# A reordered front for an embedding, interaction and MLP kernel: ids sent out by DMA broadcast from half 1 on, and new places for half 1's work

## The reference

```python
e = jnp.stack([tbl_0[ids[:, 0]], ..., tbl_15[ids[:, 15]]], axis=1)      # (2048, 16, 16)
# A = r_x0 with each of its 39 rows repeated 16 times, Bm = e stretched over the 39 rows (256 values over 39*16 places)
z = jnp.einsum('bnh,bnd,nk,khd,kd->bkh', A, Bm, alpha, w, hv[..., 0])   # (2048, 16, 16)
h = jnp.concatenate([z.reshape(2048, 256), dense_ctx], axis=1)
h = jnp.maximum(h @ W_top1 + b_top1, 0.0)                               # 272 -> 512
h = jnp.maximum(h @ W_top2 + b_top2, 0.0)                               # 512 -> 256
y = h @ W_top3                                                          # 256 -> 1
```

## Time and profile before

| | us |
|---|---|
| median of 3 runs | 192.98 (190.09 to 193.66) |
| the profiled execution | 191.44 |
| its span, from first to last instruction | 188.6 |
| TensorE busy | 170.5 (90% of the span) |
| VectorE busy | 148.1 (79%) |
| GpSimd busy | 110.9 (59%) |
| ScalarE busy | 63.2 (34%) |

### The profile page before, as it was taken

One profiled execution on the slowest core, in us unless ns is written; L12 is line 12 of the kernel. 1 busy time (PEld: TensorE's weight loads), 2 busy tenths in 40 slices (PEclk: granted clock), 3 DMA queues, 4 the chain that ended last, 5 costly groups with the idle time before them and its releaser, 6 DMA issues.

```text
span 188.6 us, 5273 instructions
## 1 busy us (share of the span) xinstructions
PE 170.5 (90%) x2238; PEld 129.6 (69%) x2238; DVE 148.1 (79%) x170; ACT 63.2 (34%) x190; POOL 110.9 (59%) x116
## 2 busy tenths in 40 slices
PE   5468497992999989999999999999999999999994
PEld 1257395682669857877787869696968786686682
DVE  3966797669379999499999997999899989777000
ACT  3275708412233212421244033412521242351232
POOL 2877777846617877662778777877777777000000
PEclk9999979999589999999999999999999999999999
DMA  4986958905869998666649794868556671000000
GB/s 72 349 257 91 256 195 265 158 6 144 211 258 346 297 359 193 148 257 228 160 80 342 244 224 123 304 202 206 187 187 168 161 225 14 2 0 3 0 0 0
DMA packets 14447, 32.62 MB, mean 173 GB/s; under 512 B 6435, under 2 KB 10320, under 8 KB 11344
## 3 DMA queue, kind: packets, MB, share of 16 engines
q1 hardware_dynamic: 9717, 29.95, 52.0%
q0 software_dynamic: 3584, 0.92, 5.1%
q10 hardware_dynamic: 1124, 1.43, 2.5%
HBM read 32.25 MB, written 0.05 MB: 171 GB/s over the span
## 4 chain that ended last, share of the span: by engine, by line
PE 80%; ACT 6%; DVE 5%; DMA 3%; issue 2%; SPq 2%; ACTq 0%; DVEq 0%
PE bank L857 18%; PE bank L789 16%; PE bank L822 14%; PE bank L795 14%; PE bank L845 5%; PE bank L782 5%; DMA table<-tbl_dram 3%; DVE e L499 2%; PE bank L880 2%; PE bank L836 2%; PE bank L866 2%; PE bank L775 2%; DVE masked L482 2%; ACT e_cols L670 2%; SPq L385 1%
## 5 line engine op out<-in xcount | busy, mean ns | idle before, releaser
L453 POOL DMA_INDIRECT e<-tbl_dram,ids_all x112 | 110.7, 988 | 48.9 <-issue 32.3
L614 DVE TENSOR_TENSOR prod<-x,bank 128x2048 f32<-128x2048 f32 x40 | 90.2, 2278 | 8.2 <-issue 4.3
L857 PE MATMUL bank<-prod,m_w 128*32 128x256 f32 x640 | 39.4, 387 | 0.0
L822 PEld LDWEIGHTS bank<-parts,onehot 125*128 125x128 bf16 x864 | 31.5, 102 | 5.2 <-issue 2.7
L822 PE MATMUL bank<-parts,onehot 125*128 125x64 bf16 (+1 forms) x864 | 33.0, 202 | 1.3 <-ACT parts L690 1.3
L789 PE MATMUL bank<-tower,w_z 128*128 128x256 f32 x128 | 31.4, 389 | 0.0
L795 PE MATMUL bank<-tower,w 128*128 128x256 f32 x128 | 30.5, 381 | 0.1
L857 PEld LDWEIGHTS bank<-prod,m_w 128*32 128x32 f32 x640 | 19.1, 111 | 14.3 <-issue 4.3
L789 PEld LDWEIGHTS bank<-tower,w_z 128*128 128x128 f32 x128 | 23.2, 190 | 5.2 <-ACT tower L694 2.7
L795 PEld LDWEIGHTS bank<-tower,w 128*128 128x128 f32 x128 | 23.3, 192 | 3.4 <-ACT tower L647 0.5
L499 DVE TENSOR_REDUCE e<-masked 128x64 f32<-128x320 f32 (+4 forms) x34 | 21.9, 665 | 0.9
(11 more groups left out here) (48 smaller groups left out, 69.3 us busy)
## 6 DMA issues: line engine op xcount, KB each, us to landing
x<-x_dram SPq DMA_DIRECT2D x16, 1024.0 KB, 8.9
x<-x_dram SPq DMA_DIRECT2D x16, 512.0 KB, 5.6
ids_b<-ids_half_dram SPq DMA_DIRECT2D x4, 576.0 KB, 7.8
e<-tbl_dram,ids_all POOLq DMA_INDIRECT x112, 4.1
prod<-windows_c_dram ACTq DMA_DIRECT2D x1, 768.0 KB, 6.4
prod<-windows_c_dram ACTq DMA_DIRECT2D x1, 512.0 KB, 4.4
w_z<-w_z_dram SPq DMA_DIRECT2D x1, 512.0 KB
w<-w_dram SPq DMA_DIRECT2D x1, 512.0 KB
```

The source lines that it names most:

```text
L453: nc.gpsimd.indirect_dma_start(out=e[:, tile, f * D:(f + 1) * D], out_offset=None, in_=t[f"tbl_{f}"][:, :], in_offset=bass.IndirectOffsetO ...
L614: nc.vector.tensor_tensor(prod[:, s % NPROD, :].rearrange("p (q b) -> p q b", q=HP), x0[:, tile % NX, :].rearrange("p (q b) -> p q b", q=H ...
L822: made = nc.tensor.matmul(o_bank[i % 2][:, at:at + m * D], onehot[:, n % 2, g, HOT.index(f), tile * P:(tile + 1) * P], parts[:, part, KT_A ...
L857: made = nc.tensor.matmul(z_bank[q * ZW:(q + 1) * ZW, a * HB:(a + 1) * HB], m_w[:, UNIT_OF[g], hp * ZW:(hp + 1) * ZW], prod[:, s % NPROD, ...
```

## The change

- The ids of the HOT tables are loaded as 72 rows (9 tables by 8 halves) of 256, not as 9 rows of 2048; `group_ids` runs once over all of them, with a per-row factor that `make_inverse` finds from the row's number.
- `PE_IDS` is 1: only half 0's ids go through TensorE and ScalarE (all five jobs in one go). From half 1 on they are stored to HBM (half 1's at once behind table pack 0, the six others later) and broadcast by DMA.
- `consts` is loaded in four pieces: identity and small constants on ScalarE's queue, the mask of 2 columns (`h8_mask`) on SyncE's; `w1_z` and `w2` have a semaphore each.
- Half 1's planes and its first pick and keep go ahead of the loop or one step up, half 2's picks to steps 5, 5, 6 and its keeps to 5, 6, 7, half 3's keeps to 9, 10, 11 (from 10, 11, 12).
- `make_mask(1, 2, NT)` moves behind `multiply(0)`. In the front, masks of two fills are made ahead of their sums. `keep_part` and `keep_ab` are interleaved in another order, and the units of `M_SUMS` too.
- The idle turns are gone.

```diff
-PLANE_STEPS = {1: [1, 1], 2: [4, 5], 3: [7, 8], ...}
-PICK_STEPS = {1: [2, 2, 3], 2: [6, 7, 7], 3: [9, 10, 11], ...}
-KEEP_STEPS = {1: [2, 3, 3], 2: [7, 8, 8], 3: [10, 11, 12], ...}
+PLANE_STEPS = {1: [BEFORE, BEFORE], 2: [4, 4], 3: [7, 8], ...}
+PICK_STEPS = {1: [BEFORE, 2, 3], 2: [5, 5, 6], 3: [9, 10, 11], ...}
+KEEP_STEPS = {1: [1, 2, 3], 2: [5, 6, 7], 3: [9, 10, 11], ...}
...
-PE_IDS = 4
-JOBS = {BEFORE: [("ids", n, j) for n in range(2) for j in range(0, len(HOT), 2)]}
+PE_IDS = 1
+JOBS = {BEFORE: [("ids", 0, j) for j in range(0, len(HOT), 2)]}
...
-IDLE_TURNS = {(0, 1): 4, (0, 2): 10, (1, 0): 10}
...
-        M_SUMS = [([4], win_bank[1]), ([0, 1], z_bank), ([2, 3], win_bank[2])]
+        M_SUMS = [([0, 1], z_bank), ([4], win_bank[1]), ([2, 3], win_bank[2])]
```

SyncE's queue:

```diff
             load_table(0)
-            sp.dma_start(consts[:], t["consts"]).then_inc(in_consts, 16)
+            sp.dma_start(h8_mask[:], t["consts"][:, AT_H_MASK:AT_H_MASK + 2]).then_inc(in_h8, 16)
             sp.dma_start(w_hv[:], t["w_hv"].rearrange("(a p) h -> p a h", p=P)).then_inc(in_w_hv, 16)
+            sp.wait_ge(ids_cast, 1)
+            sp.dma_start(ids_rows[1], ids_half[1:IDS:NH, :]).then_inc(ids_stored[0], 16)
             load_table(1)
+            sp.dma_start(ids_all[:, 2:, :], ids[:, 2:, :]).then_inc(in_ids, 16)
+            sp.wait_ge(ids_stored[0], 16)
+            load_ids(1)
             load_x0(0)
-            sp.dma_start(ids_all[:, 2:, :], ids[:, 2:, :]).then_inc(in_ids, 16)
             sp.dma_start(h4_mask[:], ...).then_inc(in_h4, 16)
+            for n in range(2, NH):
+                sp.dma_start(ids_rows[n], ids_half[n:IDS:NH, :]).then_inc(ids_stored[1], 16)
...
             sp.dma_start(b_w3[:], t["b_w3"]).then_inc(in_b_w3, 16)
+            sp.wait_ge(ids_stored[1], 16 * (NH - 2))
+            load_ids(2)
             load_x0(3)
...
             load_x0(4)
-            sp.dma_start(w2[:], t["w2"].rearrange("(a p) n -> p a n", p=P)).then_inc(in_tower, 16)
-            sp.wait_ge(ids_cast, 2)
-            sp.dma_start(ids_rows.rearrange("n f b -> f n b"), ids_half[:].rearrange("f (n b) -> f n b", b=HB)).then_inc(ids_stored, 16)
-            sp.wait_ge(ids_stored, 16)
+            sp.dma_start(w2[:], t["w2"].rearrange("(a p) n -> p a n", p=P)).then_inc(in_w2, 16)
+            load_ids(3)
```

VectorE, front and loop:

```diff
+            make_inverse()
+            group_ids()
+            dve.wait_ge(in_ids_0, 16)
+            dve.wait_ge(places_set, 1)
+            make_mask(0, 0, 2)
...
             for g in range(G):
                 make_plane(0, g, 0)
-            split_off(0, 0)
-            ...
-            make_mask(0, 0, 2)
-            split_off(0, 1)
             for g in range(G):
                 make_plane(0, g, 1)
-            dve.wait_ge(in_consts, 16)
+            split_off(0, 0)
+            split_off(0, 1)
+            split_off(1, 0)
...
-            keep_rows(0)
-            keep_rows(1)
-            for n in range(2):
-                split_off(1, n)
-            dve.wait_ge(in_ids, 16)
-            make_mask(1, 2, NT)
+            split_off(1, 1)
+            mask_rows(0)
+            mask_rows(1)
+            sum_rows(0)
+            sum_rows(1)
+            for plane in PLANES[BEFORE]:
+                make_plane(*plane)
+            mask_rows(2)
+            mask_rows(3)
+            sum_rows(2)
+            sum_rows(3)
...
             for s in range(STEPS):
                 multiply(s)
+                if s == 0:
+                    dve.wait_ge(in_ids, 16)
+                    make_mask(1, 2, NT)
                 for i in KEEPS.get(s, []):
-                    keep_rows(i)
-                if s == 1:
-                    keep_rows(2)
-                    keep_rows(3)
+                    mask_rows(i)
                 for plane in PLANES.get(s, []):
                     make_plane(*plane)
+                for i in KEEPS.get(s, []):
+                    sum_rows(i)
```

TensorE:

```diff
-                for _ in range(IDLE_TURNS.get((n, j), 0)):
-                    nc.tensor.transpose(win_bank[j][:, 0:P], ident, ident)
...
             sum_m(0)
-            turn_windows(0, 0)
-            fill_t(JOBS[BEFORE][IDS_JOBS])
-
-            pe.wait_ge(table_split, 6)
+            pe.wait_ge(table_split[1], 3)
             pick_rows(2)
             pick_rows(3)
+            turn_windows(0, 0)
             sum_m(1)
-            for job in JOBS[BEFORE][IDS_JOBS + 1:IDS_JOBS + 3]:
-                fill_t(job)
             sum_m(2)
-            for job in JOBS[BEFORE][IDS_JOBS + 3:]:
-                fill_t(job)
+            for i in PICKS[BEFORE]:
+                pick_rows(i)
...
                 if s == UH:
+                    for i in fills:
+                        pick_rows(i)
+                    turn_windows(n, 1)
                     pe.wait_ge(in_ctx, 16 * N_CTX_LOADS)
-                    pe.wait_ge(in_tower, 16 * N_TOWER_LOADS)
+                    pe.wait_ge(in_w1, 16)
+                if s == UH + 2:
+                    pe.wait_ge(in_w2, 16)
```

More of the change, by code:

```diff
@@ L295, in program @@
         in_ids_hot = sem("in_ids_hot")
-        in_row = sem("in_row")
-        in_id8 = sem("in_id8")
-        ids_stored = sem("ids_stored")
+        in_small = sem("in_small")
+        ids_stored = [sem(f"ids_stored_{n}") for n in range(2)]
         in_ids_b = {n: sem(f"in_ids_b_{n}") for n in range(PE_IDS, NH)}
-        kind_set = sem("kind_set")
         places_set = sem("places_set")
+        wide_found = sem("wide_found")
+        inverse_made = sem("inverse_made")
         ids_scaled = sem("ids_scaled")
@@ L327, in program @@
         alpha_rest = sem("alpha_rest")
-        table_split = sem("table_split")
-        table_left = sem("table_left")
+        table_split = [sem(f"table_split_{p}") for p in range(2)]
+        table_left = [sem(f"table_left_{p}") for p in range(2)]
         zeros_set = sem("zeros_set")
@@ L712, in _ @@
             act.dma_start(windows_c[:, 2:], t["windows_c"][:, 2:].bitcast(bf16)).then_inc(in_win[1], 16)
-            for job in JOBS[BEFORE][:FIRST_JOBS]:
+            for job in JOBS[BEFORE]:
                 empty(job)
             keep_part(0, 0)
-            for job in JOBS[BEFORE][FIRST_JOBS:IDS_JOBS - 1]:
-                empty(job)
-            keep_part(0, 1)
-            empty(JOBS[BEFORE][IDS_JOBS - 1])
             act.wait_ge(in_w_hv, 16)
@@ L724, in _ @@
             made.then_inc(v_made, 1)
+            keep_part(0, 1)
+            keep_part(1, 0)
+            for ft in range(2):
+                keep_ab(ft)
             keep_part(0, 2)
-            for ft in range(FT):
+            keep_part(1, 1)
+            for ft in range(2, FT):
                 keep_ab(ft)
-            keep_part(1, 0)
+            keep_part(1, 2)
+            act.wait_ge(in_h8, 16)
+            act.wait_ge(in_h4, 16)
             spread_e(0, 0)
-            keep_part(1, 1)
-            act.wait_ge(in_consts, 16)
-            act.wait_ge(in_h4, 16)
-            cut_m(0, h8_mask)
-            empty(JOBS[BEFORE][IDS_JOBS])
-            keep_part(1, 2)
-            cut_m(1, h4_mask[:])
-            for job in JOBS[BEFORE][IDS_JOBS + 1:IDS_JOBS + 3]:
-                empty(job)
+            cut_m(0, h4_mask[:])
+            cut_m(1, h8_mask[:])
+            spread_e(0, 1)
             cut_m(2, h4_mask[:])
-            for job in JOBS[BEFORE][IDS_JOBS + 3:]:
-                empty(job)
             for s in range(STEPS):
@@ L750, in _ @@
                     keep_z(n - 1)
-                if g in (0, 1):
+                if g in (0, 1) and s > 0:
                     spread_e(n, g + 1)
@@ L772, in fill_t @@
                 if kind == "ids":
-                    pe.wait_ge(ids_cast, 1 if n == 0 else 2)
+                    pe.wait_ge(ids_cast, 1)
                     for f in range(m, min(m + 2, len(HOT))):
-                        made = nc.tensor.matmul(out[0:TP, (f - m) * HB:(f - m + 1) * HB], pick[:, f:f + 1].to_broadcast([len(HOT), TP]),
-                                                ids_half[:, n * HB:(n + 1) * HB], start=True, stop=True)
+                        row = f * NH + n
+                        made = nc.tensor.matmul(out[0:TP, (f - m) * HB:(f - m + 1) * HB], pick[:, row:row + 1].to_broadcast([IDS, TP]),
+                                                ids_half[:], start=True, stop=True)
                 elif kind == "l1":
@@ L887, in _ @@
             pe.wait_ge(pick_made, 1)
-            for job in JOBS[BEFORE][:IDS_JOBS]:
+            for job in JOBS[BEFORE]:
                 fill_t(job)
@@ L951, in _ @@
                         fill_t(job)
-                if g == 0 and n > 0:
+                if g == 0 and n > 1:
                     turn_windows(n, 1)
-                if g not in (1, 3):
+                if g not in (1, 3) and s != UH:
                     for i in fills:
```

124 lines of the change are left out of this document (59 added, 65 removed).

## The result

| | before | after |
|---|---|---|
| median | 192.96 (190.09 to 193.66, 4 runs) | 181.12 (180.11 to 182.16, 4 runs) |
| profiled execution | 191.44 | 182.05 |
| its span | 188.6 | 180.2 |
| TensorE, VectorE busy | 170.5, 148.1 | 163.2, 145.2 |

The ratio is 0.9513 (95% interval 0.9461 to 0.9565). All ratios leave out runs well above the fastest ones of a kernel, so they are not the quotients of the medians. A second measurement beside other versions gave 0.9441 (0.9373 to 0.951), at 181.22 us against 190.95. The change makes the kernel 4.9 to 5.6% faster. Of the 9.4 us between the profiled executions, 8.4 lie in the span and 1.0 outside.

A forecast was written before the change was run, and what follows sets the result against it. Behind the front TensorE bounds each half at 17.9 us, so the third mark's gain is the kernel's. 8.5 us there minus 1.0 for the clock is 7.5, taking the median from 192.98 to 185.5; range 181.5 to 190.0.

The forecast's parts named there:

- the marks: Times when TensorE starts the towers of halves 0, 1 and 2; the third was forecast 8.5 us earlier than 93.92.
- VectorE's chain through the front: Masks, keeps, planes and multiplies in sequence: step 0 at 26.0, step 5 at 45.5 us against 53.11 before.
- Pack 1's first copy ahead of pack 0's third holds the picks: ScalarE's table copies in the front: picks 0 and 1 start at 16.3 us instead of 15.01, bounds 14.8 to 18.4.
- The half clock: Holes in TensorE's front drop its clock, adding 2.6 us to picks 7 and 8; 1.0 us taken off, 0.4 chance.
- Step 7 waits for the second block of windows behind layer 1: In half 0's tower: step 7 can multiply at 54.4 us, after VectorE waits 1.2 us for those windows.
- VectorE waits for pick 11, TensorE ahead of contraction 12: Between second and third mark, from half 3's earlier keeps: VectorE waits 1.9 us, TensorE 1.1 to 1.3.
- The broadcast arrives just in time: Half 1's ids, stored and broadcast in the front, land at 21.4 us, when VectorE comes to them (21.2).
- The rival's price of one for one: Slower rival, chance 0.08: each us half 1's broadcast is late counts in full; slower from 7.5 us more.
- The gain comes wholly from steps 3 and 5 no longer waiting: In the front, step 2 starts no earlier (34.4 against 33.80), step 5 at 45.5 against 53.11.
- The cold rival: Holes before step 5 drop TensorE's clock in full, with later table copies: gain about 4.7, 188.3 us; chance 0.20.
- The given-back rival: VectorE meets two more waits of 1.9 us, plus the cold restart: 2.5 us gain stays, 190.5; chance 0.13.
- the better one: Rival: table pack 1 is there at 12.5 us and picks run warm, gain about 10, 183 us; chance 0.14.

The follow-up runs named there:

- after_parts_order: Kernel after with half 3's keeps at steps 10, 11, 12 and table pack 0's third copy ahead of pack 1's first: 180.02 us, ratio 0.9376.
- after_control: Kernel after, unchanged, measured and profiled once more: 181.22 us, ratio 0.9441.
- after_keeps3_late: Kernel after with half 3's keeps at steps 10, 11, 12 as before: 180.01 us, ratio 0.9419 to the kernel before.
- after_late_broadcast: Kernel after with half 1's ids broadcast issued behind x0 tile 0, the small mask and six stores: 183.16 us, ratio 0.9578 to the kernel before.
- before_dma_ids: Kernel before with the ids of halves 2 and 3 by store and broadcast: 190.09 us, ratio 0.9916.
- before_dma_ids_split: Kernel before with ids of halves 2 and 3 by store and broadcast, and TensorE waiting for w1 at step 5, w2 at step 7: 186.74 us, ratio 0.9761.
- after_old_places: Kernel after with the old step lists for planes, picks and keeps of halves 1, 2 and 3: 187.33 us, ratio 0.9777 to the kernel before.
- before_no_turns: Kernel before without its 24 idle turns: 192.53 us, ratio 1.0068.

## Why the prediction was right, and where it wasn't

The direction was right, and the marks were: 48.2, 65.0 and 85.4 forecast, 48.65, 65.13 and 85.58 measured. That the marks agree so closely is in part luck, as the steps show:

- *Only the time until TensorE is full counts, and behind the third mark a half takes 17.9.* Right; 8.3 of the 8.4 us of the span are there at the third mark.
- *VectorE's chain through the front.* Right in shape, my times 1.1 to 1.7 us too late: step 0 at 26.0 forecast, 24.87 measured; step 5 at 45.5 and 43.80. Picks 0 and 1 started 0.7 us earlier than I had them, the planes and keeps 2 and 3 took 4.6 us (20.30 to 24.87) instead of 4.8, the masks of all halves 2.1 (27.07 to 29.14) instead of 2.3.
- *Pack 1's first copy ahead of pack 0's third holds the picks.* Right, 15.58 against 16.3 and against 15.01 before; but in the profile of after_parts_order nothing of it is left at the marks.
- *The half clock.* I took 1.0 us off for it, 0.4 of a chance of 2.6 us on picks 7 and 8. In the profiled execution it came and cost them 1.5 (4.13 instead of 2.6), since the clock rose again before they ended; in after_control it had passed before them. The marks were met with it only because the front was earlier by about as much. The two errors cancel in the marks; the 1.0 us that I took off on top of them is the term that was too much: the span gained 8.4 us where the sum said 7.5.
- *Step 7 waits for the second block of windows behind layer 1.* Wrong: step 7 multiplies the middle block, which is turned ahead of the tower, and the block behind layer 1 is for steps 8 and 9. VectorE's step 7 started at 52.46, without that wait, and step 8 at 56.39. I had reached the second mark, 65.0, through this wait on VectorE; it came at 65.13 for another reason, that TensorE was full from the first mark to the second.
- *VectorE waits for pick 11, TensorE ahead of contraction 12.* Right: 2.56 and 1.15 us, forecast 1.9 and 1.1 to 1.3, and in the chain of after_keeps3_late it is gone.
- *The broadcast arrives just in time (21.4 against 21.2).* It was earlier. SyncE's timeline has the store and the broadcast:

```profile
6.06 0.87 SPq L408 DMA_DIRECT2D ids_half_dram<-ids_half  x1
...
10.85 1.88 SPq L389 DMA_DIRECT2D ids_b<-ids_half_dram  x1
```

  From the store's issue to the broadcast's it took 4.8 us instead of the 6.9 that I had (SyncE loaded pack 1 meanwhile and waited only for the last 1.2), and the broadcast landed 5.8 us behind its issue instead of 7.8: at 16.7, with 3.6 us to spare. The rival's price of one for one is about two thirds by after_late_broadcast.
- *The gain comes wholly from steps 3 and 5 no longer waiting.* This is the reasoning that failed. before_dma_ids ended step 5's wait, with the places and the rest as before, and gained 0.8%. A product that is early is worth nothing until the tower can take its place on TensorE, and that needs w2 out of the way (2.4% with it) and the picks of half 2 in the hole before the tower; otherwise its keeps are late for the windows of step 10, and TensorE waited 2.49 us for them in before_dma_ids_split and 1.13 in after_old_places. I had read the diff's split of the semaphores and given it no price: no wait for the weights shows in the trace before, as TensorE came there only at 54.7.
- *Idle turns of 2.33 us on the chain cost more than they give.* Not shown: alone, leaving them out gave 1.0068.
- *The cold rival's 188.3.* Its own terms, 8.5 less 2.5, less 1 and less half of 2.6, leave 3.7 and not 4.7 us, which is 189.3 and no longer below the 189.1 that I called faster. The given-back rival's terms (8.5 less two times 1.9 and 2.5) leave 2.2, not 2.5.

In size, the forecast of 185.5 was 4.4 us too high, and 181.12 lies 0.4 us below its range. The clock's term is 1.0 of it. Another 1.0 is time outside the span: 2.84 us in the profiled execution of before (191.44 less 188.6), 1.85 in that of after, 1.8 in those of before_no_turns and before_dma_ids. The rest is no part of the mechanism: the median of before that I started from lay 1.5 us above its profiled execution, and that of the kernel after lies 0.9 below its own. Three later measurements of the kernel before gave 191.15, 191.81 and 190.95 us instead of 192.98, while the kernel after gave 181.12 and 181.22. Of the rivals, the better one, 183, came nearest, though for other reasons than it gave: pack 1's first copy ran at 13.51 and not at 12.5, and picks 7 and 8 ran at half clock in the profiled execution.

## What to carry to other kernels

Of a change in a front, ask where the bound engine becomes full, and what it still waits for at that point when it comes earlier: loads that were never late before can be late now, and a semaphore shared by two of them binds the early one to the late one. Parts of such a change don't add up: here the ids alone gave 0.8%, the ids with the split weights 2.4%, the whole without the new places 2.2% and without the split some 2%, and all together 5%. Work with no fixed date, like picks for a later half, belongs into a hole that stays in any case; half 2's picks are the example. And before a difference between two profiles is explained, the same kernel should be profiled twice.

## What the runs showed of the hardware

- Time from issue to landing varies much from place to place in the queue. In the kernel after, one broadcast of 576 KB landed 4.2 us behind its issue at 30.05, another 5.8 us (issue at 10.85) and another 19.0 us (issue at 51.62). From the issue of a store of ids to the end of SyncE's wait for it were 4.8 us at 6.06 in the kernel after (4.5 KB) and 6.8 us at 45.06 in the kernel before (36 KB).
- A first tower at half clock costs 5.4 to 5.5 us for 16 matmuls where it costs 3.0 at full clock. In two versions TensorE had sat idle ahead of it once, for 3.95 and 4.58 us.
- TensorE's half clock comes at other times in two executions of one kernel, with nearly the same marks: behind the first 20 us it was at 41 to 47 us in the kernel after and at 31 to 38 us in after_control, and the marks differ by 0.3 to 0.6 us.
- 40 unused transposes in TensorE's holes did not shorten the kernel. In their profile 84 pick matmuls took 2.78 us instead of 4.13, but so they did in after_control and after_keeps3_late, which have none.
